# Window attention on TensorE row groups: row scores of all four head pairs in one piece, V first in a step, and finer waits for the next image

## The chip, the cores and the metric

The kernel runs on one core of a Trainium2 chip. The metric is device time in microseconds (us), the median of several runs. Names of engines: TensorE (PE in the profile; PEld is its weight load), VectorE (DVE), ScalarE (ACT), GpSimd (POOL), SyncE (SP, which here issues all DMAs).

## The reference

The input x is 4 images of 128 channels, 112 x 112 pixels, in float32. It is normalised in 32 groups of 4 channels, rolled by (-3, -3), projected to q, k and v (one 128 x 128 matrix each, with bias), cut into windows of 7 x 7 = 49 tokens, and each window attends within itself with 8 heads of 16 channels. The result is rolled back and added to x.

```python
qkv = jnp.einsum('bchw,oc->bohw', xs, w_qkv) + b_qkv[None, :, None, None]   # xs: normalised, rolled
...
scores = jnp.einsum('bxyhqd,bxyhkd->bxyhqk', q, k) * scale
attn = jax.nn.softmax(scores, axis=-1)
out = jnp.einsum('bxyhqk,bxyhkd->bxyhqd', attn, v)
...
x = x + _L0_conv_ref(_gn(x), L0_conv_w_qkv, L0_conv_b_qkv)
```

## The kernel before

An image is 16 bands of 7 rows; a band is 16 windows, handled as two groups of 8. That makes 128 groups, g = 0 to 127, and every engine runs one step for each g. The work of a group is spread over steps: its projection and its maxima stand in step g, its softmax in step g+1, its weighting and output in steps g+2 and g+3. Five programs are written out by hand, one for each engine; each runs its own list in order, and semaphores, which count groups, join them. Nothing is scheduled by a planner, so what an engine waits for is always its next instruction in the list.

In step g, before the change:

- TensorE: `sum_keys(g-2)` (L773, the denominators), `weigh(g-2)` (L785, probabilities times V), `project_v(g)` (L705), `turn_max(g-1)` (L734, transposes the negated row maxima), `column_scores(g-1, u=0)` (L760: `scores_of_keys` L746 and then `less_maximum` L755, which subtracts the maxima), `row_scores(g, 0)` (L719), `spread_inverse(g-2)` (L798), `project_k(g+1)` (L692), `column_scores(g-1, u=1)` (first L755, then L746), `row_scores(g, 1)`, `project_q(g+1)` (L699).
- ACT: `evac_q(g)` (L364), `normalise(g+2)` (L352), `evac_even(g-2)` (L392), `high_inverse(g-2)` (L386), `evac_neg(g-1)` (L370), `evac_v(g)` (L381), `exp(g-1, 0)` (L375), `evac_k(g+1)` (L359), `exp(g-1, 1)`.
- DVE: `low_q(g)`, `invert(g-2)`, `mask_q(g)`, `low_inverse(g-2)` (L581), `join(g-2)` (L590), `maximum(g, 0)` (L571), a chunk of the next image's statistics (`take_stats`, L491), `scale_rows(g-2)` (L597), `maximum(g, 1)`.
- POOL: `split_max(g-1)`, `add_image(g-3)`, `split_x(g+2)`, `split_k(g+1)`.

The scores are made twice: once with queries on the partitions (`row_scores`, 100 rows by 49 keys), only to find each row's maximum, and once with keys on the partitions (`column_scores`), which the exponential reads. A row score is one matmul that uses 32 rows of the array (the 32 channels of a pair of heads) and all 128 columns, with 49 moving columns. There are 8 windows, 3 products of high and low halves, and 4 head pairs h: 96 matmuls in a step. Head pair h lies on array rows 32h to 32h+31. Before the change each call handles two head pairs, which write two PSUM banks (0 and 1), and the second call waits until DVE has read the maxima of the first:

```python
wait(pe, max_done[1 - j], g + j)
for w in range(GW):
    for n, (low, k) in enumerate(((0, k_hi), (0, k_lo), (Q_LEN, k_hi))):
        for h in (2 * j, 2 * j + 1):
```

PSUM has 8 banks: 0 and 1 row scores (bank 0 also the turned maxima), 2 and 3 column scores (3 also the denominators), 4 Q and K, 5 V and the spread inverse, 6 and 7 the weighted result (`OUT_BANKS`), which `evac_even` and `join` read.

SP stores a finished band and then loads the band of the image after next into the freed slot. DVE takes the statistics of image b+1 while image b is worked on, 28 chunks of 448 pixels. After a change of image, in step 32b+2, DVE waits for all 16 bands of image b+1 (`dve.wait_ge(loaded[b + 1], 32 * BANDS)`), the last of which is loaded only when the last band of image b-1 has been stored.

## Time and profile before

| | |
|---|---|
| median of 3 runs | 1049.76 us (1048.53 to 1051.95) |
| profiled execution, its own time | 1047.67 us |
| its span, first to last instruction | 1045.9 us |
| mean granted TensorE clock | 0.970 |
| PE busy | 976.6 us (93%), 46595 matmuls |
| DVE busy | 785.8 us (75%) |
| ACT busy | 697.1 us (67%) |
| POOL busy | 595.6 us (57%) |
| HBM read and written | 25.89 MB and 25.69 MB |

The busy times are unions of the records of an engine over the whole span. The matmuls' records overlap, since a record holds the pipeline's latency as well as the stream of columns; the distance between starts tells what a matmul costs TensorE. The three runs lie 3.4 us apart (0.3%).

### The profile page before, as it was taken

The page shows a single profiled execution, that of the slowest core. Times are in us where ns is not written, and L with a number is a line of the kernel's source. Part 1 is how long each engine was busy: PE and PEld are TensorE (multiplying, and loading weights), DVE is VectorE, ACT ScalarE, POOL GpSimd, SP SyncE. Part 2 cuts the span into 40 slices and gives each one's busy share as a digit, 9 for nine tenths or more (in the row PEclk, how much of TensorE's full clock was granted, in tenths as well). Part 3 has the DMA queues.
Part 4 walks back from the last instruction along what each step waited for, and adds up shares of the span by engine and source line. Part 5 has one row for each costly group of instructions (what it writes and reads, how often), then busy time and mean ns, then how long its engine had stood idle before and what let it go on. Part 6 is the DMA issues. An engine that isn't in the chain of part 4 may idle for free. (4 is left out here: it accounts for less than half of the span.)

```text
span 1045.9 us, 104658 instructions
## 1 busy us (share of the span) xinstructions
PE 976.6 (93%) x46595; PEld 770.2 (74%) x46595; DVE 785.8 (75%) x1532; ACT 697.1 (67%) x1297; POOL 595.6 (57%) x1067
## 2 busy tenths in 40 slices
PE   0589999999979999999997999999999999999995
PEld 0367777777767777777775777787878787777774
DVE  7656888889856888888984888788877777777762
ACT  2455777777756777777774777777777777777752
POOL 1444666666555665666663666566656665666651
PEclk9988999999998999999997999999999999999995
DMA  9201111111110111111110000000000000000000
GB/s 382 119 18 52 47 45 61 61 54 39 61 62 31 61 40 53 61 61 46 46 62 31 31 31 15 31 31 31 15 31 31 31 19 27 31 31 24 22 33 34
DMA packets 29925, 52.05 MB, mean 50 GB/s; under 512 B 3650, under 2 KB 28868, under 8 KB 29764
## 3 DMA queue, kind: packets, MB, share of 16 engines
q1 hardware_dynamic: 29892, 51.59, 14.0%
q8 instruction: 23, 0.38, 0.2%
q14 instruction: 10, 0.08, 0.0%
HBM read 25.89 MB, written 25.69 MB: 49 GB/s over the span
## 5 line engine op out<-in xcount | busy, mean ns | idle before, releaser
L571 DVE TENSOR_REDUCE neg_max<-psum 100x16 f32<-100x784 f32 x256 | 249.5, 975 | 172.3 <-PE psum L729 172.3
L375 ACT ACTIVATE probs_t<-psum,exp_scale 128x800 f32<-128x800 f32 x256 | 237.5, 928 | 85.6 <-PE psum L746 55.4
L283 POOL TENSOR_SCALAR k_hi<-k 128x392 f16<-128x392 f32 x128 | 67.5, 527 | 243.3 <-PE psum L746 242.0
L746 PE MATMUL psum<-q_masks,k_hi 32*64 32x100 f16 x8192 | 190.3, 208 | 15.8 <-DVE inv L576 12.4
L729 PE MATMUL psum<-k_hi,q_masks 32*128 32x49 f16 x8192 | 199.2, 180 | 2.3 <-issue 1.2
L305 POOL TENSOR_TENSOR stage<-mixed,image 128x343 f32 (+7 forms) x256 | 162.4, 653 | 48.4 <-issue 37.4
L729 PEld LDWEIGHTS psum<-k_hi,q_masks 32*128 32x128 f16 x8192 | 176.4, 91 | 12.0 <-issue 1.6
L729 PE MATMUL psum<-k_lo,q_masks 32*128 32x49 f16 x4096 | 183.6, 179 | 0.6 <-issue 0.6
L746 PEld LDWEIGHTS psum<-q_masks,k_hi 32*64 32x64 f16 x8192 | 153.7, 106 | 39.1 <-issue 16.9
L564 DVE TENSOR_SCALAR q_masks<-q_halves,even_odd 128x800 f16<-128x800 f16 x256 | 162.8, 678 | 0.1
L729 PEld LDWEIGHTS psum<-k_lo,q_masks 32*128 32x128 f16 x4096 | 161.8, 92 | 0.8 <-issue 0.8
L746 PE MATMUL psum<-q_masks,k_lo 32*64 32x100 f16 x4096 | 160.7, 205 | 0.7 <-issue 0.7
L352 ACT ACTIVATE xn<-image,shift_c,rstd_c 128x21 f32 (+6 forms) x256 | 131.4, 564 | 8.8 <-DVE exp_scale L479 7.0
L793 PE MATMUL psum<-probs_t,v_rows 64*32 64x100 f32 x8192 | 133.3, 255 | 2.8 <-issue 2.8
L779 PEld LDWEIGHTS psum<-probs_t,sum_rows 128*32 128x32 f32 x8192 | 102.3, 112 | 45.0 <-issue 44.9
L285 POOL TENSOR_TENSOR k_lo<-k,k_hi 128x392 f16<-128x392 f32 x128 | 116.3, 909 | 10.7
L275 POOL TENSOR_TENSOR xn_lo<-xn,xn_hi 128x392 f16<-128x392 f32 x128 | 116.3, 908 | 10.7
L779 PE MATMUL psum<-probs_t,sum_rows 128*32 128x49 f32 x8192 | 120.1, 211 | 1.6 <-ACT probs_t L375 1.1
L746 PEld LDWEIGHTS psum<-q_masks,k_lo 32*64 32x64 f16 x4096 | 120.1, 107 | 1.0 <-issue 1.0
L556 DVE SCALAR_TENSOR_TENSOR q_halves<-psum,q_bias,q_halves 128x392 f16<-128x392 f32 x128 | 80.4, 628 | 51.7 <-ACT q_halves L364 36.6
L359 ACT ACTIVATE k<-psum,k_bias 128x392 f32<-128x392 f32 x128 | 75.2, 588 | 65.1 <-PE psum L696 65.1
L392 ACT ACTIVATE even_out<-psum,v_scale 128x392 f32<-128x392 f32 x128 | 75.2, 587 | 57.1 <-PE psum L793 57.1
(120 smaller groups left out, 1909.9 us busy)
## 6 DMA issues: line engine op xcount, KB each, us to landing
out_dram<-stage SPq DMA_DIRECT2D x64, 224.0 KB, 2.0
out_dram<-stage SPq DMA_DIRECT2D x64, 168.0 KB, 1.9
image<-in_x_dram SPq DMA_DIRECT2D x32, 224.0 KB, 2.6
image<-in_x_dram SPq DMA_DIRECT2D x1, 6104.0 KB, 27.2
image<-in_x_dram SPq DMA_DIRECT2D x34, 168.0 KB, 2.5
image<-in_x_dram SPq DMA_DIRECT2D x6, 896.0 KB, 9.4
image<-in_x_dram SPq DMA_DIRECT2D x1, 728.0 KB, 14.0
w_nat<-in_L_conv_w_qkv_dram SPq DMA_DIRECT2D x1, 192.0 KB, 2.5
```

The costliest lines, as they stand in the source:

```text
L275: nc.gpsimd.tensor_tensor(xn_lo[:, par, :, 0:TOK], xn[:, :, :], xn_hi[:, par, :, 0:TOK], ALU.subtract).then_inc(x_split, 1)
L285: nc.gpsimd.tensor_tensor(k_lo[:, par, :, 0:TOK], k, k_hi[:, par, :, 0:TOK], ALU.subtract).then_inc(k_split, 1)
L305: last = nc.gpsimd.tensor_tensor(pixel_view(stage[:, bass.ds(st, BAND)], piece), token_view(mixed[:, half, :, :], piece), pixel_view(image ...
L352: last = nc.scalar.activation(token_view(xn, piece), pixel_view(image[:, bass.ds(at, BAND)], piece), ACT.Identity, bias=shift_c[:, 0:1], s ...
L375: nc.scalar.activation(probs_t[:, 2 * u:2 * u + 2, :, :].rearrange("p h a q -> p h (a q)"), psum[:, COL_BANKS, 0:PAIRS * ROWS2], ACT.Exp, ...
L556: nc.vector.scalar_tensor_tensor(q_halves[:, 1, :, 0:TOK], psum[:, QK_BANK, 0:GT].rearrange("p (w q) -> p w q", q=TOK), q_bias[:, 0:1], q_ ...
L564: last = nc.vector.tensor_scalar(both[:, :, e, :], q_halves[:, :, :, :].rearrange("p l w q -> p (l w) q"), even_odd[:, e:e + 1], None, ALU ...
L571: nc.vector.tensor_reduce(neg_max[:, par, 2 * j:2 * j + 2, :], psum[0:ROWS2, ROW_BANKS, 0:GT] .rearrange("p h (w k) -> p h w k", k=TOK), A ...
L729: last = nc.tensor.matmul(psum[:, ROW_BANKS.start + h - 2 * j, w * TOK:(w + 1) * TOK], q_masks[rows, par, low + w * ROWS2:low + w * ROWS2 ...
L746: last = nc.tensor.matmul(psum[side, COL_BANKS.start + h % 2, a * ROWS2:(a + 1) * ROWS2], k[rows, par, w, :], q_masks[rows, par, low + w * ...
L779: last = nc.tensor.matmul(psum[c * PC:(c + 1) * PC, SUM_BANK, SPARE_SUM], sum_rows[:, a, e, :, :, :].rearrange("p t w s -> p (t w s)"), pr ...
L793: last = nc.tensor.matmul(psum[c * PC:(c + 1) * PC, OUT_BANKS.start + s, a * ROWS2:(a + 1) * ROWS2], v_rows[side, par, a, c * PC:(c + 1) * ...
```

## The change

- `row_scores(g)` is one call over all four head pairs. Pairs 0 and 1 write banks 6 and 7, pairs 2 and 3 banks 0 and 1. Since banks 6 and 7 also hold the weighted result, `row_scores(g)` waits for `join(g-2)`, and `weigh(g-2)` waits for `maximum(g-1, 0)`. (DVE raises `join_done` and `mixed_done` once at the start, so that their counts are one higher everywhere.)
- TensorE's list: `project_v(g)` comes first in a step, then `sum_keys` and `weigh`; `row_scores(g)` stands behind `project_k(g+1)`.
- ACT's list: `evac_v(g)` comes second. DVE's list: statistics and `scale_rows` stand ahead of both maxima.
- At an image change DVE's waits for loaded bands are cut in four, each for the bands that the next two chunks need; the wait for all 16 comes in step 32b+6 in place of 32b+2.
- At the start ACT waits for `scales_ready` only after its first step, statistics begin in step 2 rather than 1, and TensorE's loop begins at step 2, not 4, so that two steps less are written out.

```diff
@@ window_attention
-        ROW_BANKS, COL_BANKS, OUT_BANKS = slice(0, 2), slice(2, 4), slice(6, 8)
+        ROW_BANKS, COL_BANKS, OUT_BANKS = (slice(6, 8), slice(0, 2)), slice(2, 4), slice(6, 8)
...
-        row_mm = [sem("row_mm_0"), sem("row_mm_1")]
+        row_mm = sem("row_mm")
@@ scalar (ACT)
-            act.wait_ge(scales_ready, 1)
-
...
             def step(g, n, par):
                 if live(g):
                     evac_q(g)
+                    evac_v(g, par)
                 if live(g + 2):
                     normalise(g + 2, n + 1, par)
                 if live(g - 2):
...
                     high_inverse(g - 2)
                 if live(g - 1):
                     evac_neg(g - 1)
-                if live(g):
-                    evac_v(g, par)
-                if live(g - 1):
                     exp(g - 1, 0)
...
             act.wait_ge(norm_ready, 1)
-            for g in range(-2, 4):
+            step(-2, -1, 0)
+            act.wait_ge(scales_ready, 1)
+            for g in range(-1, 4):
                 step(g, g // 2, g & 1)
@@ vector (DVE)
+            dve.sem_inc(join_done, 1)
+            dve.sem_inc(mixed_done, 1)
...
             def maximum(g, par, j):
-                dve.wait_ge(row_mm[j], g + 1)
+                dve.wait_ge(row_mm, g + 1)
                 wait(dve, neg_split, g - 1)
-                nc.vector.tensor_reduce(neg_max[:, par, 2 * j:2 * j + 2, :], psum[0:ROWS2, ROW_BANKS, 0:GT]
+                nc.vector.tensor_reduce(neg_max[:, par, 2 * j:2 * j + 2, :], psum[0:ROWS2, ROW_BANKS[j], 0:GT]
...
                     join(g - 2)
                 if before:
                     before()
+                for chunk in chunks:
+                    take_stats(image_at + chunk * STAT, chunk)
+                if live(g - 2):
+                    scale_rows(g - 2, par)
+                if after:
+                    after()
                 if live(g):
                     maximum(g, par, 0)
-                for chunk in chunks:
-                    take_stats(image_at + chunk * STAT, chunk)
-                if after:
-                    after()
-                if live(g - 2):
-                    scale_rows(g - 2, par)
-                if live(g):
                     maximum(g, par, 1)
...
             step(0, 0, 0)
+            step(1, 0, 1)
             dve.wait_ge(loaded[1], 32)
-            step(1, 0, 1, (0, 1), BANDS * BAND)
-            step(2, 1, 0, (2, 3), BANDS * BAND)
-            step(3, 1, 1, (4, 5), BANDS * BAND)
+            step(2, 1, 0, (0, 1, 2), BANDS * BAND)
+            step(3, 1, 1, (3, 4, 5), BANDS * BAND)
...
-                dve.wait_ge(loaded[b + 1], 32 * -(-2 * STAT // BAND))
-                two_steps(first, 0, at)
-                dve.wait_ge(loaded[b + 1], 32 * -(-4 * STAT // BAND))
-                two_steps(first + 1, 2, at)
+                for n in range(4):
+                    dve.wait_ge(loaded[b + 1], 32 * -(-(2 * n + 2) * STAT // BAND))
+                    two_steps(first + n, 2 * n, at)
                 dve.wait_ge(loaded[b + 1], 32 * BANDS)
-                with dve.Fori(2, CHUNKS // 2) as n:
+                with dve.Fori(4, CHUNKS // 2) as n:
                     two_steps(n + first, 2 * n, at)
@@ tensor (PE)
-            def row_scores(g, par, j):
-
-                if j == 0:
-                    pe.wait_ge(q_masked, g + 1)
-                    pe.wait_ge(k_split, g + 1)
-                wait(pe, max_done[1 - j], g + j)
+            def row_scores(g, par):
+                pe.wait_ge(q_masked, g + 1)
+                pe.wait_ge(k_split, g + 1)
+                wait(pe, max_done[1], g)
+                wait(pe, join_done, g)
                 for w in range(GW):
                     for n, (low, k) in enumerate(((0, k_hi), (0, k_lo), (Q_LEN, k_hi))):
-                        for h in (2 * j, 2 * j + 1):
+                        for h in range(HP):
                             rows = slice(h * PC, (h + 1) * PC)
-                            last = nc.tensor.matmul(psum[:, ROW_BANKS.start + h - 2 * j, w * TOK:(w + 1) * TOK],
+                            last = nc.tensor.matmul(psum[:, ROW_BANKS[h // 2].start + h % 2, w * TOK:(w + 1) * TOK],
...
             def weigh(g, par):
                 pe.wait_ge(v_evac, g + 1)
-                wait(pe, join_done, g)
+                pe.wait_ge(max_done[0], min(g + 2, GROUPS) if isinstance(g, int) else g + 2)
+                wait(pe, join_done, g + 1)
...
+                if live(g):
+                    project_v(g, par)
                 if live(g - 2):
                     sum_keys(g - 2)
                     weigh(g - 2, par)
-                if live(g):
-                    project_v(g, par)
                 if live(g - 1):
                     turn_max(g - 1)
                     column_scores(g - 1, 1 - par, 0)
-                if live(g):
-                    row_scores(g, par, 0)
                 if live(g - 2):
                     spread_inverse(g - 2, live(g))
                 if live(g + 1):
                     project_k(g + 1, 1 - par)
+                if live(g):
+                    row_scores(g, par)
                 if live(g - 1):
                     column_scores(g - 1, 1 - par, 1)
-                if live(g):
-                    row_scores(g, par, 1)
                 if live(g + 1):
                     project_q(g + 1, 1 - par)
 
-            for g in range(-1, 4):
+            for g in range(-1, 2):
                 step(g, g & 1)
-            with pe.Fori(2, GROUPS // 2 - 1) as n:
+            with pe.Fori(1, GROUPS // 2 - 1) as n:
```

TensorE, loop body, before: from the end of `column_scores(g-1, 0)` to `column_scores(g-1, 1)`. L755 is `less_maximum`, L729 `row_scores`, L805 `spread_inverse`, L696 `project_k`. The brackets name the semaphores waited for.

```order
L755 MATMUL psum<-neg_rows,pick_window 128x100 [waits neg_ready]
L755 MATMUL psum<-neg_rows,pick_window 128x100 x7
L729 MATMUL psum<-k_hi,q_masks 128x49 [waits max_done_1,k_split,q_masked]
L729 MATMUL psum<-k_hi,q_masks 128x49
L729 MATMUL psum<-k_lo,q_masks 128x49 x2
L729 MATMUL psum<-k_hi,q_masks 128x49 x4
...
L805 MATMUL psum<-inv_rows,pick_head 128x49 [waits v_evac,inv_split]
L805 MATMUL psum<-inv_rows,pick_head 128x49 x7
```

The same place after the change (L752, L803, L694 and L726 are the same four functions):

```order
L752 MATMUL psum<-neg_rows,pick_window 128x100 [waits neg_ready]
L752 MATMUL psum<-neg_rows,pick_window 128x100 x7
L799 REGISTER_ALU [waits inv_split]
L803 MATMUL psum<-inv_rows,pick_head 128x49 [waits v_evac]
L803 MATMUL psum<-inv_rows,pick_head 128x49 x7
...
L726 MATMUL psum<-k_hi,q_masks 128x49 [waits max_done_1,join_done,k_split,q_masked]
L726 MATMUL psum<-k_hi,q_masks 128x49 x3
L726 MATMUL psum<-k_lo,q_masks 128x49 x4
L726 MATMUL psum<-k_hi,q_masks 128x49 x8
...
L752 MATMUL psum<-neg_rows,pick_window 128x100 [waits exp_done_0]
```

The row scores moved behind `project_k`, are issued in fours in place of twos, and gained the wait for `join_done`.

TensorE at the start of a step, before: `sum_keys` L779, `weigh` L793, `project_v` L710 and L714, `turn_max` L736.

```order
L779 MATMUL psum<-probs_t,sum_rows 32x49 [waits exp_done_1,exp_done_0]
L779 MATMUL psum<-probs_t,sum_rows 32x49 x31
L793 MATMUL psum<-probs_t,v_rows 32x100 [waits v_evac,join_done]
L793 MATMUL psum<-probs_t,v_rows 32x100 x31
L710 MATMUL psum<-bias_rows,ones_rows 128x512 [waits mixed_done,v_evac]
...
L736 MATMUL psum<-ident,neg_halves 128x100 [waits neg_split]
```

And after (`project_v` L708, `sum_keys` L776, `weigh` L791, `turn_max` L733, first row of `scores_of_keys` L743):

```order
L708 MATMUL psum<-bias_rows,ones_rows 128x512 [waits mixed_done,v_evac]
...
L776 MATMUL psum<-probs_t,sum_rows 32x49 [waits exp_done_1,exp_done_0]
L776 MATMUL psum<-probs_t,sum_rows 32x49 x31
L791 MATMUL psum<-probs_t,v_rows 32x100 [waits join_done,v_evac,max_done_0]
L791 MATMUL psum<-probs_t,v_rows 32x100 x31
L733 MATMUL psum<-ident16,neg_halves 128x100 [waits neg_split]
L743 MATMUL psum<-q_masks,k_hi 64x100 [waits inv_done,exp_done_1]
```

`project_v` no longer lies between `weigh` and `turn_max`; `weigh` now also waits for the first maxima of the group before.

ACT, one step of its loop, before and then after (L392/L390 `evac_even`, L386/L384 `high_inverse`, L370/L368 `evac_neg`, L381/L379 `evac_v`):

```order
L392 ACTIVATE even_out<-psum,v_scale 128x392 [waits join_done,out_mm]
L386 CAST inv_hi<-inv 128x49 [waits inv_split,inv_done]
L370 CAST neg_rows<-psum 128x100 [waits col_mm_1,neg_mm]
L381 COPY v_rows<-psum 128x512 [waits out_mm,v_mm]
L375 ACTIVATE probs_t<-psum,exp_scale 128x800 [waits out_mm,col_mm_0]
```

```order
L379 COPY v_rows<-psum 128x512 [waits out_mm,v_mm]
...
L390 ACTIVATE even_out<-psum,v_scale 128x392 [waits join_done,out_mm]
L384 CAST inv_hi<-inv 128x49 [waits inv_split,inv_done]
L368 CAST neg_rows<-psum 128x100 [waits col_mm_1,neg_mm]
L373 ACTIVATE probs_t<-psum,exp_scale 128x800 [waits out_mm,col_mm_0]
```

`evac_v` left its place between `evac_neg` and the exponential; `evac_even` and `high_inverse` still stand ahead of `evac_neg`.

## Rows read from the trace of the kernel before

**Rows 1.** Busy time in a stretch: us, then PE, PEld, DVE, ACT, POOL, clock, DMA
```profile
600.00:1000.00 400.00, 400.00 (x19600) 317.02 (x19606) 311.49 (x585) 290.46 (x538) 248.85 (x431) 1.00 0.07 27
```

**Rows 2.** Source line L710 (once a step), 600 to 1000 us: first and last start
```profile
L710 PE MATMUL psum<-bias_rows,ones_rows x54: 390/390/390, 599.8 to 993.4; 128*128 128x512 f16 x54
```

**Rows 3.** Timeline of TensorE, one step: start, us, engine, line, operation
```profile
857.97 0.91 PE L779 MATMUL psum<-probs_t,sum_rows 128*32 128x49 f32 x64
858.81 1.02 PE L793 MATMUL psum<-probs_t,v_rows 64*32 64x100 f32 x64
859.76 0.39 PE L710 MATMUL psum<-bias_rows,ones_rows 128*128 128x512 f16 x1
...
860.65 0.21 PE L736 MATMUL psum<-ident,neg_halves 100*128 100x100 bf16 x1
860.79 0.24 PE L746 MATMUL psum<-q_masks,k_hi 32*64 32x100 f16 x4
...
861.45 0.35 PE L755 MATMUL psum<-neg_rows,pick_window 32*128 32x100 bf16 x8
861.63 0.19 PE L729 MATMUL psum<-k_hi,q_masks 32*128 32x49 f16 x2
...
862.21 0.18 PE L729 MATMUL psum<-k_hi,q_masks 32*128 32x49 f16 x2
862.33 0.37 PE L805 MATMUL psum<-inv_rows,pick_head 128*128 128x49 f16 x8
862.54 0.33 PE L696 MATMUL psum<-xn_hi,w_hi 128*128 128x392 f16 x1
...
863.14 0.35 PE L755 MATMUL psum<-neg_rows,pick_window 32*128 32x100 bf16 x8
863.42 0.24 PE L746 MATMUL psum<-q_masks,k_hi 32*64 32x100 f16 x4
...
864.08 0.20 PE L729 MATMUL psum<-k_hi,q_masks 32*128 32x49 f16 x2
...
864.78 0.34 PE L702 MATMUL psum<-xn_hi,w_hi 128*128 128x392 f16 x1
...
865.40 0.29 PE L779 MATMUL psum<-probs_t,sum_rows 128*32 128x49 f32 x8
```

**Rows 4.** Timeline of ACT in the same step
```profile
859.94 0.59 ACT L392 ACTIVATE even_out<-psum,v_scale 128x392 f32<-128x392 f32 x1 [0.64 <-PE psum L793]
860.43 0.23 ACT L386 CAST inv_hi<-inv 128x49 f16<-128x49 f32 x1
860.90 0.24 ACT L370 CAST neg_rows<-psum 128x100 bf16<-128x100 f32 x1 [0.25 <-PE psum L736]
861.04 0.59 ACT L381 COPY v_rows<-psum 128x512 f32<-128x512 f32 x1
861.84 0.93 ACT L375 ACTIVATE probs_t<-psum,exp_scale 128x800 f32<-128x800 f32 x1 [0.21 <-PE psum L755]
```

**Rows 5.** Timeline of DVE in the same step
```profile
860.84 0.26 DVE L581 SCALAR_TENSOR_TENSOR inv_rows<-inv_hi,low_rows,inv 128x49 f16<-128x49 f16 x1
861.02 0.74 DVE L590 SCALAR_TENSOR_TENSOR summed<-psum,v_scale,even_out 128x196 f32<-128x196 f32 x2
```

**Rows 6.** Image changes: DVE's timeline at the first; L710 at first and second
```profile
310.64 0.63 DVE L556 SCALAR_TENSOR_TENSOR q_halves<-psum,q_bias,q_halves 128x392 f16<-128x392 f32 x1 [7.45 <-DMA image<-in_x_dram]
...
L710 PE MATMUL psum<-bias_rows,ones_rows x2: 389/389/389, 304.5 to 321.9; 128*128 128x512 f16 x2
...
L710 PE MATMUL psum<-bias_rows,ones_rows x3: 390/390/390, 544.7 to 570.1; 128*128 128x512 f16 x3
```

**Rows 7.** Start of the kernel: source line L710, first seven steps
```profile
L710 PE MATMUL psum<-bias_rows,ones_rows x7: 389/390/627, 39.1 to 96.6; 128*128 128x512 f16 x7
```

**Rows 8.** Busy time in stretches, columns as in the first group
```profile
75.00:81.00 6.00, 5.05 (x215) 3.81 (x203) 3.61 (x9) 2.96 (x6) 2.51 (x5) 1.00 0.44 136
...
82.00:88.00 6.00, 5.96 (x213) 4.65 (x213) 2.65 (x5) 2.71 (x5) 2.88 (x5) 0.50 0.02 6
```

More of the change, by code:

```diff
@@ L389, in evac_even @@
                 act.wait_ge(out_mm, g + 1)
-                wait(act, join_done, g)
+                wait(act, join_done, g + 1)
                 even = psum[:, OUT_BANKS, 0:PAIRS * ROWS2].rearrange("p s (a e q) -> p s a e q", e=2, q=QP)[:, :, :, 0, 0:TOK]
@@ L585, in join @@
                 dve.wait_ge(even_done, g + 1)
-                wait(dve, mixed_done, g)
+                wait(dve, mixed_done, g + 1)
                 by_side = summed[:, :, :].rearrange("p (a s) q -> p s a q", s=2)
@@ L802, in spread_inverse @@
                 else:
[L803 removed]
+                    pe.wait_ge(mixed_done, g + 1)
                 for w in range(GW):
```

9 lines of the change are left out of this document (4 added, 5 removed).

## The prediction

> **What bounds the kernel now.** I read the busy times of a quiet stretch first. Between 600 and 1000 us TensorE is busy for 400.00 of 400 us at granted clock 1.00, DVE for 311.49, ACT for 290.46 [rows 1]. So TensorE sets the pace there, and DVE, which needs 78% of a step, could follow a step of 5.8 us. The length of a step comes from a line that is issued once in each: L710 starts 54 times from 599.8 to 993.4, 53 steps of 7.43 us [rows 2]. Then I read TensorE's timeline for one step, by distances between starts, since these and not the records' lengths are what it pays [rows 3]. Block by block: sum_keys 0.84, weigh 0.95, project_v 0.89, turn_max 0.14, keys of column score 0 0.66, its less_maximum 0.18, row score 0 0.70, spread_inverse and project_k together 0.81, less_maximum 0.28, keys of column score 1 0.66, row score 1 0.70, project_q 0.62. The sum is 7.43, with no wait in it.
>
> The span of 1045.9 us is then: 118 steps of 7.43, two long ones at image changes, a slow start and a tail. The profiled execution took 1047.7 us; the median of the runs is 2.1 us above it, which I add at the end.
>
> **Row scores in fours.** One piece has 48 matmuls, in pairs on two groups of 32 array rows. The first pair starts at 861.63 and the 24th at 862.21, so 23 pairs take 0.58 us: 25 ns a pair [rows 3]. The next block, which uses the array in another shape, starts 0.12 after the last pair, 0.10 more than a pair needs. I count 0.10 for such a change of shape, included in the blocks above.
>
> After the change the 96 matmuls are 24 fours. What a four costs no row shows. Below: 25 ns, if four row groups run beside each other as two do now. Above: 50 ns, if nothing is won over two pairs, and more if four outputs at once get in each other's way. Three neighbours speak for the low end. spread_inverse issues 8 matmuls of the same 49 columns with full 128 x 128 weights in 0.21 us, 26 ns each [rows 3], so the weights of all four row groups go in within 26 ns. The keys of a column score are 48 matmuls in 0.66 less 0.10, that is 11.7 ns each, with 100 columns and four tiles beside each other [rows 3]; so issuing costs at most 11.7 ns and four would be at most 47. And the columns alone, 49 at 2.4 GHz, need 20.4 ns, the same for two or four groups. I take 25 ns: row scores cost 24 x 0.025 = 0.60 in place of 1.20.
>
> A rule speaks against this. The Trainium skill, TensorEngine Tiling, section Instruction Overhead, says that each matmul has an overhead of some 60 cycles and that a tiling factor should not be taken from a dimension that is already small. Our 49 columns are such a dimension, and 60 cycles are 25 ns. The trace agrees on the size, but shows it for a pair and not for one matmul [rows 3], so the floor is one of a row group. By the rule, paid matmul after matmul, the row scores would take 2.4 us and the sum would come to some 1200 us, which two groups already contradict.
>
> **Changes of shape.** Before there are ten in a step. After, row score and less_maximum (both 32 x 128) and project_q and project_v (both full) are neighbours, and project_v parts from turn_max by sum_keys and weigh: nine. That saves 0.10. TensorE's own work falls to 7.43 - 0.60 - 0.10 = 6.73 us.
>
> **The wait that takes its place.** project_v used to stand between weigh and turn_max and gave ACT 0.89 us in which to get through. Count from the start of the new step, at project_v. It takes 0.89 + 0.10 (shape), sum_keys until 1.83, weigh until 2.78, turn_max until 2.92, keys of column score 0 until 3.58. There less_maximum needs neg_rows from ACT. evac_even starts 1.13 us after weigh starts (859.94 less 858.81), so at 2.96; high_inverse follows 0.49 later at 3.45; evac_neg can follow 0.14 after that (the distance of two such short instructions is that of 860.90 and 861.04) and lasts 0.24: 3.83 [rows 3, 4]. A semaphore's reach from TensorE to ACT is 0.04 (turn_max ends at 860.86, evac_neg starts at 860.90) and I take 0.05 for the way back: 3.88. TensorE waits 0.30 us, in every step. Moving evac_v ahead does not help here, since evac_even waits for weigh and not for ACT.
>
> What follows is not late. less_maximum lasts 0.18 + 0.10, until 4.16. spread_inverse needs DVE's low_inverse: inv_hi is done at 3.68, low_inverse starts at 3.72 and ends at 3.98 [rows 4, 5]. Then 0.81 until 4.97. There the new wait for join: join starts 0.18 after low_inverse, 3.90, and ends at 4.64 [rows 5], 0.33 early. Behind the row scores (5.57) column score 1 needs the first exponential: it starts 0.39 after less_maximum starts (861.84 less 861.45) and lasts 0.93, so it ends at 5.20 [rows 3, 4], 0.37 early. Then 0.28, 0.66 and project_q with 0.62 less 0.10: the step ends at **7.03 us**, 0.40 less than now. DVE's 5.8 us with the statistics ahead of the maxima fit: all of its list but the maxima lies beside TensorE's first 5.6 us, and the maxima beside column score 1, project_q and the next project_v. weigh's new wait, for a maximum that is read some 2 us after the row scores, ends before the 1.83 + 7.03 - 5.57 = 3.3 us that TensorE takes to get there.
>
> **Image changes.** DVE waits 7.45 us for the DMA at the first, and L710, normally 7.43 apart, is 17.4 apart there; at the second, two periods take 25.4 [rows 6]. Beyond a normal step that is 10.0 and 10.5, wait and slow restart together. In the new code the wait for all bands stands four steps (28 us) later, and the bands of the first four waits were loaded long before. The third change has no such wait. I take all 20.5 us as gained. The instructions that merge statistics stand ahead of the maxima now; they have the slack of DVE, some 1.2 us a step, and I count them at nothing (at most 1 us for each of three changes).
>
> **Start.** The first six periods of L710 take 57.5 us against 44.6 for six normal ones: 12.9 too many [rows 7]. Part of it is code that is met for the first time, which before are steps 0 to 3 written out and then two of the loop, and after 0 and 1 and two of the loop. I take a third of 12.9 as gained, 4.3 (estimate; 0 to 10). ACT's later wait and the rest of the DVE prologue: not counted, under 1 us.
>
> **Sum.** Steps: 118 normal ones and the six first, 124 x 0.40 = 49.6. Image changes 20.5. Start 4.3. In all 74.4: 1047.7 - 74.4 = 973.3, and with the 2.1 of the median **975 us**.
>
> **Rivals.** The fixed part, 24.8 us, holds in all of them; what differs is the step, P, and the time is 1049.8 - 24.8 - 124 x (7.43 - P).
>
> - The main case: P from 6.93 to 7.15, 963 to 990 us with the steps alone, 956 with a start at its better end. Chance 0.72.
> - Fours at 25 ns, but another wait of 0.1 to 0.4 us in each step. The list of candidates is above: join has 0.33 of slack, the exponential 0.37, low_inverse 0.18, and ACT's three-piece normalise of every other group lies just ahead of evac_even. P 7.15 to 7.45: 990 to 1027 us. 0.14.
> - Four row groups win little: a four at 47 to 50 ns. P is 7.03 + 24 x 0.025 = 7.63 at 50, and the 0.20 that each step loses eats exactly the fixed part: 1050 us. At 47 it is 1041. For it speaks that no row has more than two groups of rows writing all 128 columns at once. 0.07.
> - The other side: the two further groups are served in turn, one after the other, behind the first pair, since each of the four writes every partition of PSUM. A four then costs 25 + 25 + 25 = 75 ns, row scores 1.80, P = 8.23: 1124 us. It decides from 50 ns a four on. Against it: two groups that write all partitions show no such price. 0.04.
> - The clock. Now 84% busy at 75 to 81 us is followed by 0.50 of the clock at 82 to 88, where 6 us hold 213 matmuls against 49 a microsecond in the quiet stretch [rows 1, 8]. The new step leaves TensorE idle for 0.30 of 7.03 us, 96% busy. Should 0.50 be granted in the middle of the run, a step takes about 1.4 times as long by these counts (35 a microsecond), 3 us more; from 25 such steps on the gain is gone. The Trainium skill, TensorE: Matmul & The Clock Gate, Part 1, tells of a kernel whose frequent short idle times between groups of matmuls made the clock swing. 0.03.
>
> **How the numbers follow.** Faster by over 0.3% (about what a measurement of this kernel can tell from no change): the first two and most of the third, 0.91. Within 0.3%: the top of the third, 0.02. Slower: the last two, 0.07. The range takes in the main case and the nearer half of the second: 956 to 1006 us, 0.80.
>
> **What the new profile would show.** Right: 96 row-score matmuls within 0.60 us, starts of fours 25 ns apart; L708 starting every 7.03 us; before L752, the first less_maximum of a step, an idle time of TensorE's weight load of 0.3 us ended by ACT's neg_rows; no DVE wait for a DMA at the image changes and steps there as long as others; granted clock 1.00 from the fourth step on. The prediction is wrong if fours are 40 ns or more apart, if the wait stands before L726 with DVE's summed as its releaser, or if the clock row of the quiet stretch is below 1.00.

## The result, and the profile after

The changed kernel takes 1367.03 us (median of 4 runs, 1366.01 to 1369.11), the kernel before 1050.12 beside it. The ratio is 1.302, between 1.299 and 1.305: 317 us slower, where 75 us faster was forecast. The forecast missed by 392 us. One of the four runs of e6 below took 1532.40 us, for a reason that nothing here shows; it is part of e6's median of 1011.41 us, which would be 1010.94 without it, and its ratio leaves it out.

The page of the kernel after, its span, busy times and clock row:

```profile
span 1363.9 us, 104634 instructions
PE 1115.8 (82%) x46595; PEld 847.6 (62%) x46595; DVE 751.7 (55%) x1532; ACT 668.7 (49%) x1297; POOL 588.0 (43%) x1067
PEclk9887787787787787787787787787787787787786
```

The same work stands there, 46595 matmuls, but no engine is full. The clock row is the surprise: 7 and 8 through the whole run. Busy time in the stretch that [rows 1] showed full (us; then PE, PEld, DVE, ACT, POOL, clock, DMA):

```profile
600.00:1000.00 400.00, 338.02 (x14213) 257.35 (x14214) 230.13 (x478) 203.00 (x396) 179.23 (x315) 0.80 0.07 26
```

TensorE is idle for 62 of 400 us, and the clock granted to it averages 0.80. `project_v`'s first matmul, once a step, from 600 to 900 us:

```profile
L708 PE MATMUL psum<-bias_rows,ones_rows x29: 377/378/628, 604.8 to 891.6; 128*128 128x512 f16 x29
```

29 starts from 604.8 to 891.6 are 28 steps of 10.24 us, against 7.43 [rows 2] and 7.03 forecast. The waits of the whole run: engine, line and what it waited for, then us in total, times, longest us (three rows of the list):

```profile
ACT v_rows L379 <- PE psum L791: 336.0, 126, 3.8
DVE inv_rows L581 <- ACT inv_hi L384: 237.4, 128, 2.9
PE psum L752 <- ACT neg_rows L368: 193.5, 125, 1.9
```

The three rows belong together. ACT stands for 336 us, 2.7 us in each step, before `evac_v`, until TensorE's `weigh` (L791) is done. So what ACT does behind it, `inv_hi` and `neg_rows` among it, comes late. DVE waits for `inv_hi`, and TensorE stands before `less_maximum` (L752) for `neg_rows`, 1.55 us a step. It is the only wait that TensorE has in every step. Here is ACT's timeline: start, us, engine, line, operation, and in brackets the idle time ahead and what ended it:

```profile
607.71 0.58 ACT L379 COPY v_rows<-psum 128x512 f32<-128x512 f32 x1 [1.86 <-PE psum L791]
608.19 0.75 ACT L350 ACTIVATE xn<-image,shift_c,rstd_c 128x392 f32 x1
608.84 0.58 ACT L390 ACTIVATE even_out<-psum,v_scale 128x392 f32<-128x392 f32 x1
609.31 0.23 ACT L384 CAST inv_hi<-inv 128x49 f16<-128x49 f32 x1
609.43 0.25 ACT L368 CAST neg_rows<-psum 128x100 bf16<-128x100 f32 x1
...
618.86 0.58 ACT L379 COPY v_rows<-psum 128x512 f32<-128x512 f32 x1 [3.61 <-PE psum L791]
619.34 1.30 ACT L350 ACTIVATE xn<-image,shift_c,rstd_c 128x343 f32 x3
...
621.13 0.24 ACT L368 CAST neg_rows<-psum 128x100 bf16<-128x100 f32 x1
```

And TensorE's, from the row scores ahead of the first of these steps on, with the wait of the second step as its last row:

```profile
602.62 0.20 PE L726 MATMUL psum<-k_hi,q_masks 32*128 32x49 f16 x4
602.68 0.21 PE L726 MATMUL psum<-k_hi,q_masks 32*128 32x49 f16 x8
...
603.39 0.34 PE L752 MATMUL psum<-neg_rows,pick_window 32*128 32x100 bf16 x8
...
606.66 1.02 PE L791 MATMUL psum<-probs_t,v_rows 64*32 64x100 f32 x64
607.61 0.22 PE L733 MATMUL psum<-ident,neg_halves 100*128 100x100 bf16 x1
...
609.74 0.35 PE L752 MATMUL psum<-neg_rows,pick_window 32*128 32x100 bf16 x8 [1.26 <-ACT neg_rows L368]
...
621.43 0.52 PE L752 MATMUL psum<-neg_rows,pick_window 32*128 32x100 bf16 x8 [1.86 <-ACT neg_rows L368]
```

Read the two together. `weigh` has issued its last matmul when `turn_max` starts at 607.61, and `evac_v` starts 0.10 later, 607.71. In [rows 4] it was `evac_even` that started at `weigh`'s end. Now `evac_v` (0.48 until the next start), `normalise` (0.65) and `evac_even` (0.47) stand in a row between `weigh` and `neg_rows`, and in every other group `normalise` has three pieces and takes 1.30, so that the wait is 1.86 and not 1.26. `evac_v(g)` waits for `weigh(g-2)` since `v_rows` has two buffers and `weigh` reads the one that is overwritten: `wait(act, out_mm, g - 1)`. That wait was there before too, but there it stood behind `evac_even`, which waits for the same event, and cost nothing.

Also seen here: 96 row-score matmuls take 0.77 us (602.62 to 603.39), not 0.60. Stretches of 3 us show how the clock goes in the middle of the run, columns as above:

```profile
612.00:615.00 3.00, 3.00 (x69) 1.90 (x60) 1.85 (x2) 1.26 (x2) 1.18 (x2) 0.50 0.19 69
...
618.00:621.00 3.00, 1.57 (x113) 1.23 (x89) 0.91 (x3) 2.14 (x5) 0.13 (x1) 1.00 0.00 0
```

0.50, the lower of the two levels (1.2 GHz), is granted from 612 to 615 us, behind the wait that ends at 609.74, and 1.00 (2.4 GHz) is back at 618 to 621; the kernel before kept 1.00 in its quiet stretch [rows 1].

### The profile page after: what moved, and what is told of

The parts are those of the page before. It is cut to its first block and busy times, and to the rows that moved or that the text cites. A ratio compares the mean times of both kernels' runs of the same rounds, so it can differ in the third digit from the quotient of the medians.

```text
span 1363.9 us, 104634 instructions
## 1 busy us (share of the span) xinstructions
PE 1115.8 (82%) x46595; PEld 847.6 (62%) x46595; DVE 751.7 (55%) x1532; ACT 668.7 (49%) x1297; POOL 588.0 (43%) x1067
## 5 line engine op out<-in xcount | busy, mean ns | idle before, releaser
L752 PE MATMUL psum<-neg_rows,pick_window 32*128 32x100 bf16 x2048 | 108.9, 238 | 194.1 <-ACT neg_rows L368 193.5
L379 ACT COPY v_rows<-psum 128x512 f32<-128x512 f32 x128 | 74.9, 585 | 337.4 <-PE psum L791 336.0
L743 PE MATMUL psum<-q_masks,k_hi 32*64 32x100 f16 x8192 | 217.1, 225 | 3.3 <-issue 3.3
L752 PEld LDWEIGHTS psum<-neg_rows,pick_window 32*128 32x128 bf16 x2048 | 66.7, 109 | 211.4 <-ACT neg_rows L368 210.5
L743 PEld LDWEIGHTS psum<-q_masks,k_hi 32*64 32x64 f16 x8192 | 177.7, 119 | 27.0 <-issue 7.4
L273 POOL TENSOR_SCALAR xn_hi<-xn 128x392 f16<-128x392 f32 x128 | 67.4, 527 | 292.0 <-ACT xn L350 292.0
L743 PE MATMUL psum<-q_masks,k_lo 32*64 32x100 f16 x4096 | 184.1, 222 | 1.0 <-issue 1.0
L581 DVE SCALAR_TENSOR_TENSOR inv_rows<-inv_hi,low_rows,inv 128x49 f16<-128x49 f16 x128 | 35.1, 274 | 237.4 <-ACT inv_hi L384 237.4
L726 PEld LDWEIGHTS psum<-k_hi,q_masks 32*128 32x128 f16 x8192 | 125.4, 106 | 63.2 <-issue 62.6
L776 PE MATMUL psum<-probs_t,sum_rows 128*32 128x49 f32 x8192 | 146.4, 237 | 2.2 <-ACT probs_t L373 2.2
L726 PE MATMUL psum<-k_hi,q_masks 32*128 32x49 f16 x8192 | 141.7, 205 | 2.1 <-issue 2.1
L776 PEld LDWEIGHTS psum<-probs_t,sum_rows 128*32 128x32 f32 x8192 | 127.2, 132 | 21.5 <-issue 15.0
L791 PE MATMUL psum<-probs_t,v_rows 64*32 64x100 f32 x8192 | 134.3, 256 | 0.3 <-issue 0.3
L576 DVE RECIPROCAL inv<-psum 128x49 f32<-128x49 f32 x128 | 60.1, 470 | 134.6 <-PE psum L776 134.6
L743 PEld LDWEIGHTS psum<-q_masks,k_lo 32*64 32x64 f16 x4096 | 132.3, 119 | 1.1 <-issue 1.1
L726 PE MATMUL psum<-k_lo,q_masks 32*128 32x49 f16 x4096 | 131.1, 204 | 2.0 <-issue 2.0
```

Of the source, the lines that this page charges most:

```text
L273: nc.gpsimd.tensor_scalar(xn_hi[:, par, :, 0:TOK], xn[:, :, :], 1.0, 0.0, ALU.mult, ALU.add).then_inc(x_high, 1)
L379: nc.scalar.copy(v_rows[:, par, :, :].rearrange("p a d -> p (a d)"), psum[:, V_BANK, :]).then_inc(v_evac, 1)
L726: last = nc.tensor.matmul(psum[:, ROW_BANKS[h // 2].start + h % 2, w * TOK:(w + 1) * TOK], q_masks[rows, par, low + w * ROWS2:low + w * RO ...
L743: last = nc.tensor.matmul(psum[side, COL_BANKS.start + h % 2, a * ROWS2:(a + 1) * ROWS2], k[rows, par, w, :], q_masks[rows, par, low + w * ...
L752: last = nc.tensor.matmul(psum[:, COL_BANKS.start + h % 2, a * ROWS2:(a + 1) * ROWS2], pick_window[rows, 2 * a:2 * a + 2, :].rearrange("p ...
L776: last = nc.tensor.matmul(psum[c * PC:(c + 1) * PC, SUM_BANK, SPARE_SUM], sum_rows[:, a, e, :, :, :].rearrange("p t w s -> p (t w s)"), pr ...
```

## Experiments

The theory after the result (A): the wait for `out_mm`, moved ahead of `normalise`, `evac_even` and `evac_neg` with `evac_v`, makes TensorE idle, and the idle time costs the clock. Rivals: (B) ACT merely has more work ahead of `neg_rows`, the wait is nothing; (C) four row groups at once are slow; (D) the new waits that tie `weigh` and `row_scores` to DVE's maxima and `join`. In each diff "-" is the kernel that it starts from. Ratios are to the kernel before, run beside it, with their 95% interval.

**e1, the copy back.** The changed kernel, with ACT's `evac_v` where it stood before.

```diff
                     evac_q(g)
-                    evac_v(g, par)
...
                     evac_neg(g - 1)
+                if live(g):
+                    evac_v(g, par)
```

> The changed kernel with one thing undone: ACT's evac_v stands behind evac_neg again, as before the change. Theory (ACT): in the changed order evac_v is ACT's second instruction and waits not only for project_v but, by its wait for out_mm, for weigh of the group two back, whose buffer it overwrites; normalise, evac_even, high_inverse and evac_neg queue behind it, so that TensorE waits 1.3 us (even groups) or 1.9 us (odd groups) in front of less_maximum, and these idle times make the granted clock fall. With evac_v back, the wait before less_maximum should be 0.3 us, one of 0.2 us should appear before spread_inverse (it needs evac_v), the step should be 7.4 us and the clock 1.00 in the middle of the run: 1022 us, 1010 to 1040. Rival (row groups): the clock falls because four row groups run at once, whatever ACT does: clock stays near 0.80, the step above 8.5 us, time above 1180.

Measured: 1038.28 us, 0.9884 (0.9866 to 0.9903). One line moved takes off 329 us, so (C) and (D) are out as causes of the loss. The stretch of 600 to 900 us, then who waited before `less_maximum`, then the first matmul of `project_v`:

```profile
600.00:900.00 300.00, 279.12 (x14444) 217.38 (x14437) 251.25 (x439) 203.56 (x398) 183.20 (x319) 1.00 0.07 27
...
PEld psum L754 <- ACT neg_rows L368: 10.8, 39, 0.3
...
L710 PE MATMUL psum<-bias_rows,ones_rows x40: 377/377/378, 601.2 to 896.3; 128*128 128x512 f16 x40
```

The wait of 0.30 that the prediction worked out is there: 10.8 us in 39 steps. But the step is 7.57, not 7.03, and my 1022 was missed. Single steps alternate between 7.31 and 7.84. The cause of the long ones shows below (e8).

**e11, the wait alone.** e1, and at the place where the changed kernel has `evac_v`, ACT waits for the same semaphore and copies nothing.

```diff
                     evac_q(g)
+                    wait(act, out_mm, g - 1)
+                    act.sem_inc(waited_act, 1)
```

> The copy-back kernel (evac_v behind evac_neg, 1038 us) with the wait alone put where the change puts it: ACT waits for weigh of the group two back behind evac_q, without copying anything there. Theory (the wait and what queues behind it): normalise, evac_even, high_inverse and evac_neg start only after weigh, the wait before less_maximum is 0.9 us (even groups) and 1.5 (odd), the clock falls below 0.95 and the time is above 1150 us. Rival (the half microsecond of the copy and its place): no change, 1030 to 1050 us.

Measured: 1367.11 us, 1.3025 (1.300 to 1.305), the changed kernel's time. The busy row, then `turn_max` and `normalise` in one step, then the waits of the next:

```profile
600.00:900.00 300.00, 254.97 (x10695) 192.79 (x10699) 174.47 (x348) 151.76 (x292) 132.58 (x234) 0.79 0.08 28
...
607.41 0.22 PE L737 MATMUL psum<-ident,neg_halves 100*128 100x100 bf16 x1
607.89 0.75 ACT L350 ACTIVATE xn<-image,shift_c,rstd_c 128x392 f32 x1 [2.23 <-PE psum L795]
...
620.97 0.35 PE L756 MATMUL psum<-neg_rows,pick_window 32*128 32x100 bf16 x8 [1.56 <-ACT neg_rows L368]
621.54 0.36 PE L807 MATMUL psum<-inv_rows,pick_head 128*128 128x49 f16 x8 [0.22 <-ACT v_rows L379]
```

So the wait gives the loss without the copy, and (B), by which the wait is nothing, is out. It doesn't follow that the copy's 0.48 us is worth nothing. Nothing is copied here ahead of `normalise`, and yet it starts 0.48 after `turn_max` (607.41 to 607.89), where the changed kernel has 0.58 (607.61 to 608.19): the bare wait takes most of the copy's time. And the copy, now behind `neg_rows`, makes `spread_inverse` wait for `v_rows`. That the two times agree so closely is in part luck. What the copy is worth shows in e3.

**e2, four buffers.** The wait goes away by rights when `v_rows` has four buffers, since then `weigh(g-4)` frees the one that is written.

```diff
-        v_rows = sb("v_rows", [C, 2, PAIRS, C])
+        v_rows = sb("v_rows", [C, 4, PAIRS, C])
...
-                wait(act, out_mm, g - 1)
+                wait(act, out_mm, g - 3)
...
-            with pe.Fori(1, GROUPS // 2 - 1) as n:
-                step(2 * n, 0)
-                step(2 * n + 1, 1)
+            with pe.Fori(0, (GROUPS // 2 - 2) // 2) as m:
+                for i in range(4):
+                    step(4 * m + 2 + i, i & 1, i)
```

> The changed kernel in its own order, but v_rows has four buffers in place of two, so that evac_v of a group waits for weigh of four groups back and not of two (loops of ACT and TensorE hold four steps instead of two). Theory (ACT's wait): evac_v no longer waits for TensorE's weigh of this step; wait before less_maximum 0.3 us for even and odd groups alike, step 7.2 us, clock 1.00: 997 us, 985 to 1015. Rival (position): the copy's place and its 0.5 us on ACT make less_maximum late even without the wait: a wait above 0.7 us, step above 7.6, time above 1046. Rival (row groups): clock near 0.80 and above 1180 us.

Measured: 1571.86 us, 1.494 (1.490 to 1.498). This run doesn't decide what it was made for, since it changed something else. Its queue that loads instructions (packets, MB, share), and two of TensorE's waits over the whole run, at the row scores and before `less_maximum`:

```profile
q8 instruction: 413, 6.77, 1.9%
...
PE psum L730 <- issue: 108.9, 92, 2.5
...
PE psum L756 <- ACT neg_rows L368: 6.7, 39, 0.2
```

In the changed kernel that queue has 17 packets and 0.28 MB and the wait for "issue" at the row scores is 4.0 us in place of 108.9. The buffer's number is a constant in this kernel's code, so the loops hold four steps in place of two; that TensorE's longer body is loaded anew in each pass is my reading of the 6.77 MB. The wait for `neg_rows` does fall from 193.5 to 6.7 us, but TensorE is itself late here, which gives ACT time. How much of the run's time is the loading stays open.

**e3, normalise first.** The changed kernel with `evac_v` behind `normalise`, so that this is done by the time `weigh` ends.

```diff
                     evac_q(g)
-                    evac_v(g, par)
                 if live(g + 2):
                     normalise(g + 2, n + 1, par)
+                if live(g):
+                    evac_v(g, par)
```

> The changed kernel with normalise ahead of evac_v on ACT, a smaller dose: normalise runs while evac_v's wait for weigh lasts, but evac_v itself (0.49 us) still stands ahead of evac_even and evac_neg. Theory: wait before less_maximum 0.8 us for even and odd groups alike, a tenth of a step. If TensorE keeps its clock at 10% idle time, the step is 7.7 us and the time 1058 (1045 to 1075); if the clock falls at 10% too, it is above 1150. Rival (row groups): same clock, near 0.80, as the changed kernel.

Measured: 1147.9 us, 1.0932 (1.091 to 1.095).

```profile
600.00:900.00 300.00, 265.76 (x12932) 205.72 (x12920) 229.24 (x405) 183.44 (x354) 162.80 (x284) 0.93 0.06 23
...
PE psum L753 <- ACT neg_rows L368: 23.0, 35, 0.7
```

The wait before `less_maximum` falls to 0.66 us a step, and the clock comes back to 0.93, between my two cases (1058 with it, over 1150 without). Less than half of that wait is left, and 219 us of the time are gone. Beside e1 this is the price of the copy. Here `evac_v` waits for the same `weigh` as the `evac_even` behind it, so all that its place adds is 0.48 us ahead of `neg_rows`, and e3 takes 110 us more than e1. Taken in this order, and with what the clock makes of them, the 329 us have two parts: 110 for the copy in that place, and 219 for the wait that pushes `normalise` behind `weigh`.

**e5, filler.** What is the clock's share? The changed kernel, with 28 matmuls that write unused columns of a bank, placed ahead of the wait before `less_maximum`. They compute nothing, and hold TensorE busy while `neg_rows` is late (the wait for `q_low` is there so that nothing else uses the bank).

```diff
+                        pe.wait_ge(q_low, g + 2)
+                        for _ in range(FILL):
+                            nc.tensor.matmul(psum[:, QK_BANK, GT:GT + ROWS2], w_hi[:, 1, :], w_hi[:, 0, 0:ROWS2], ...)
```

> The changed kernel with 28 extra matmuls a step on TensorE (full array, 100 columns, into free columns of the Q/K bank, result unused), issued just ahead of less_maximum's wait for ACT, some 1.25 us of work that lies inside the time in which TensorE waits there anyway. It adds work and removes none. Theory (idle time sets the clock): the clock stays at 1.00, the wait left is 0 to 0.1 us (even groups) and 0.6 us (odd), the step is 8.5 us on average and the time 1160 us (1130 to 1190), some 200 faster than the changed kernel by doing more. Rival (row groups or load make the clock fall): clock 0.80 or lower and 1367 us or more.

Measured: 1161.26 us, 1.1057 (1.104 to 1.108).

```profile
600.00:900.00 300.00, 290.58 (x13792) 236.51 (x13775) 211.52 (x404) 178.29 (x353) 160.66 (x282) 1.00 0.07 24
...
608.98 0.22 PE L734 MATMUL psum<-ident,neg_halves 100*128 100x100 bf16 x1
...
609.78 1.41 PE L766 MATMUL psum<-w_hi 128*128 128x100 f16 x28
611.12 0.35 PE L753 MATMUL psum<-neg_rows,pick_window 32*128 32x100 bf16 x8
...
L709 PE MATMUL psum<-bias_rows,ones_rows x35: 377/377/377, 606.2 to 896.2; 128*128 128x512 f16 x35
```

More work takes 206 us off. The clock is 1.00, and the step, 34 in 290.0 us, is 8.53. The filler takes next to no time of its own: `less_maximum` starts 2.14 after `turn_max` (608.98 to 611.12), in the changed kernel 2.13 (607.61 to 609.74). So of the 392 us of the miss, 206 are the clock; a step of 8.53 in place of 7.03 is the rest, 124 x 1.50 = 186. Of the 1.50, the wait is 1.25 (1.55 less the 0.30 forecast) and the row scores 0.17; 0.08 I don't assign.

**e4, image changes alone.** The kernel before, with only DVE's finer waits for loaded bands.

```diff
-                dve.wait_ge(loaded[b + 1], 32 * -(-2 * STAT // BAND))
-                two_steps(first, 0, at)
-                dve.wait_ge(loaded[b + 1], 32 * -(-4 * STAT // BAND))
-                two_steps(first + 1, 2, at)
+                for n in range(4):
+                    dve.wait_ge(loaded[b + 1], 32 * -(-(2 * n + 2) * STAT // BAND))
+                    two_steps(first + n, 2 * n, at)
```

> The kernel before with the change's waits for loaded bands at an image change and nothing else of it. The prediction's term: the two long steps at image changes (10.0 and 10.5 us beyond a normal one) go entirely, 1050.5 - 20.5 = 1030 us (1027 to 1033). Rival: the wait is only put off, and DVE waits in step 32b+6 for the last band, or the merging of statistics becomes late: above 1040 us.

Measured: 1027.76 us, 0.9798 (0.976 to 0.983), 21.1 below the 1048.86 of the kernel before beside it. `project_v` at the first image change:

```profile
L709 PE MATMUL psum<-bias_rows,ones_rows x6: 389/389/389, 297.1 to 334.2; 128*128 128x512 f16 x6
```

Five steps of 7.42: the long one is gone. The term of 20.5 holds, and it is a gain by itself.

**e6, a new order.** Can the order of the whole be had without the wait? On ACT `evac_even` and `evac_v` go behind `evac_neg`, so nothing that waits for `weigh` stands ahead of it; on TensorE `project_k` goes ahead of `spread_inverse`, which then has 0.5 us more for `low_inverse`. From e1:

```diff
@@ scalar (ACT)
-                    evac_even(g - 2)
                     high_inverse(g - 2)
                 if live(g - 1):
                     evac_neg(g - 1)
+                if live(g - 2):
+                    evac_even(g - 2)
@@ tensor (PE)
-                if live(g - 2):
-                    spread_inverse(g - 2, live(g))
                 if live(g + 1):
                     project_k(g + 1, 1 - par)
+                if live(g - 2):
+                    spread_inverse(g - 2, live(g))
```

> The changed kernel with another order on ACT and one exchange on TensorE. ACT: evac_q, normalise, high_inverse, evac_neg, evac_even, evac_v, exp 0, evac_k, exp 1; TensorE: project_k ahead of spread_inverse. Neither evac_neg nor high_inverse stands behind an instruction that waits for weigh, and evac_v's half microsecond is over before spread_inverse, now later, needs it. Theory: no wait of TensorE above 0.1 us in a step, clock 1.00, a step of 6.9 us (6.73 and 0.17 for row scores that take 0.77 and not 0.60): 1050 - 25 - 124 x 0.5 = 963 us, 955 to 985. Rival (a chain that I don't see, or DVE held by GpSimd as in the copy-back run): a step above 7.2, above 996 us.

Measured: 1011.41 us, 0.9623 (0.958 to 0.967), against 963 expected. Steps alternate between 6.90 and 7.76: one in two is what was hoped for. In a long one TensorE waits twice for DVE, for `low_inverse` and then for `join`, which stands behind it in DVE's list:

```profile
611.69 0.37 PE L806 MATMUL psum<-inv_rows,pick_head 128*128 128x49 f16 x8 [0.26 <-DVE inv_rows L584]
612.44 0.20 PE L729 MATMUL psum<-k_hi,q_masks 32*128 32x49 f16 x4 [0.37 <-DVE summed L593]
```

**e8, GpSimd's reads.** The long steps of e1 and e6 have a long `low_inverse`. Here it is in a short and in a long step of e1, then what GpSimd does beside the long one, then TensorE behind it:

```profile
604.95 0.40 DVE L583 SCALAR_TENSOR_TENSOR inv_rows<-inv_hi,low_rows,inv 128x49 f16<-128x49 f16 x1 [0.24 <-ACT inv_hi L384]
...
612.38 0.92 DVE L583 SCALAR_TENSOR_TENSOR inv_rows<-inv_hi,low_rows,inv 128x49 f16<-128x49 f16 x1
...
612.32 0.91 POOL L275 TENSOR_TENSOR xn_lo<-xn,xn_hi 128x392 f16<-128x392 f32 x1
...
613.35 0.37 PE L805 MATMUL psum<-inv_rows,pick_head 128*128 128x49 f16 x8 [0.67 <-DVE inv_rows L583]
```

The same instruction took 0.26 in [rows 5]. The long one ends 0.07 after GpSimd's subtraction, and TensorE waits 0.67 for it. e8 is e1 with that subtraction done for one window of eight (the low half of the normalised input is zero in the others, so part of the products is left out).

```diff
-                nc.gpsimd.tensor_tensor(xn_lo[:, par, :, 0:TOK], xn[:, :, :], xn_hi[:, par, :, 0:TOK],
+                nc.gpsimd.tensor_tensor(xn_lo[:, par, 0:1, 0:TOK], xn[:, 0:1, :], xn_hi[:, par, 0:1, 0:TOK],
```

> The copy-back kernel with GpSimd's xn_lo subtraction done for one of the 8 windows only (the rest of the low half of x stays zero, which leaves a part of the products out). In the copy-back run every other step was 7.85 and not 7.31 us, and in it DVE's low_inverse took 0.92 us in place of 0.27 and ended 0.07 after GpSimd's xn_lo. Theory (a shared way to SBUF holds DVE while GpSimd reads): low_inverse takes 0.3 us in all steps, both kinds of step are 7.31, and the time is 124 x 0.27 less: 1005 us (998 to 1015). Rival (low_inverse is long for ACT's sake or for the odd groups' three-piece normalise): steps go on alternating and the time stays within 8 us of 1038.

Measured: 1013.95 us, 0.9674 (0.963 to 0.972), 24 below e1. The long steps go from 7.84 to 7.42. `low_inverse`, grouped by line (count, total us and mean ns of one; then idle ahead), in e1 and in e8:

```profile
L583 DVE SCALAR_TENSOR_TENSOR inv_rows<-inv_hi,low_rows,inv 128x49 f16<-128x49 f16 x128 | 81.6, 638 | 21.1 <-ACT inv_hi L384 20.6
```

```profile
L583 DVE SCALAR_TENSOR_TENSOR inv_rows<-inv_hi,low_rows,inv 128x49 f16<-128x49 f16 x128 | 45.9, 358 | 20.4 <-ACT inv_hi L384 19.9
```

The Trainium skill, SBUF — State Buffer, section Who interferes with whom, states that a DVE instruction with two SBUF inputs contends with a GpSimd instruction that reads SBUF, and that one with at most one such input doesn't, outside DVE's 2-port modes. The first half is what these rows show; the second half is a remedy, tried next.

**e10, the inverse in PSUM.** e6, with the reciprocals written to free columns of PSUM bank 1, so that `low_inverse` has one SBUF input.

```diff
-        inv32 = sb("inv32", [C, TOK])
+        inv32 = psum[:, 1, GT:GT + TOK]
```

> e6_new_order with the reciprocals of the denominators (inv32) in free columns of PSUM bank 1 in place of SBUF, so that DVE's low_inverse reads one input from SBUF and not two. In e6_new_order every other step was 7.76 and not 6.90 us, and in it low_inverse started 0.06 after GpSimd's xn_lo and ended 0.06 after it (0.92 us). Theory (DVE is held when it needs a second SBUF input while GpSimd reads): low_inverse takes 0.3 us throughout, all steps are 6.9 to 7.0 us, and the time is 124 x 0.43 = 53 us less than 1011: 960 (950 to 975). Rival: the odd step is long for another reason and the time stays above 1000.

Measured: 970.63 us, 0.9247 (0.923 to 0.926), the fastest of all and 79 us below the kernel before. `low_inverse` in e6 and then in e10:

```profile
L584 DVE SCALAR_TENSOR_TENSOR inv_rows<-inv_hi,low_rows,inv 128x49 f16<-128x49 f16 x128 | 72.2, 564 | 0.6 <-ACT inv_hi L384 0.6
```

```profile
L584 DVE SCALAR_TENSOR_TENSOR inv_rows<-inv_hi,low_rows,psum 128x49 f16<-128x49 f16 x128 | 32.6, 255 | 0.5 <-ACT inv_hi L384 0.5
```

From 564 to 255 ns, with GpSimd's work whole. Its stretch and steps:

```profile
600.00:900.00 300.00, 296.50 (x15628) 238.09 (x15616) 251.43 (x468) 215.73 (x430) 195.96 (x342) 1.00 0.08 28
...
L711 PE MATMUL psum<-bias_rows,ones_rows x42: 377/377/378, 605.8 to 893.1; 128*128 128x512 f16 x42
```

TensorE is busy for 296.50 of 300 us, and 41 steps take 287.3: 7.01 each. The expected 960 (950 to 975) was met.

**e7 and e9, pairs for fours.** What are the fours worth? e7 was to be e6 with the row scores in two runs of pairs, as the expectation says.

```diff
-                    for n, (low, k) in enumerate(((0, k_hi), (0, k_lo), (Q_LEN, k_hi))):
-                        for h in range(HP):
+                    for j, n, (low, k) in ((j, *t) for j in range(2) for t in enumerate(((0, k_hi), (0, k_lo), (Q_LEN, k_hi)))):
+                        for h in (2 * j, 2 * j + 1):
```

> The same kernel as e6_new_order, but the 96 row-score matmuls are issued in pairs (all of head pairs 0 and 1, then all of 2 and 3), in one piece. Theory: pairs cost 25 ns as before the change, 1.20 us in place of 0.77, TensorE is the bound, so the step is 0.43 longer than in e6_new_order and the time 50 us longer (40 to 60). Rival: the step is bound elsewhere, and fours gain less than 15 us over pairs.

Measured: 1013.83 us, 0.9657 (0.963 to 0.969), 2.4 above e6. That wasn't the experiment described: the pairs change inside each window, and one pair runs beside the other; the 96 matmuls took 0.80 us (601.39 to 602.19 in one step). e9 is the real one, on e10, with all of pairs 0 and 1 ahead of pairs 2 and 3:

```diff
-                for w in range(GW):
+                for j, w in ((j, w) for j in range(2) for w in range(GW)):
...
-                        for h in range(HP):
+                        for h in (2 * j, 2 * j + 1):
```

> e10_inverse_psum with the row scores as two runs of pairs, first all windows of head pairs 0 and 1, then all of 2 and 3, which is how the kernel before issues them; e7_pairs changed head pairs inside each window, so that pairs of different row groups still overlapped (its 96 matmuls took 0.79 us). Theory: 96 matmuls take 1.20 us at 25 ns a pair, TensorE is the bound and the step is 0.43 longer: 45 to 60 us more than e10_inverse_psum. Rival: less than 20 us more, fours do not pay.

Measured: 1015.32 us, 0.9668 (0.965 to 0.969), 44.7 above e10.

```profile
L711 PE MATMUL psum<-bias_rows,ones_rows x41: 377/377/378, 603.9 to 898.6; 128*128 128x512 f16 x41
```

Steps of 7.37 against 7.01. The fours are worth 0.36 a step, where 0.60 was forecast, and 44.7 us lies just under the 45 to 60 that I expected.

## Why the prediction was wrong

**The step that failed** is in the part on the wait: "Moving evac_v ahead does not help here, since evac_even waits for weigh and not for ACT." It looks at what `evac_v` leaves behind and not at what it takes along. The chain was started with `evac_even` 1.13 after `weigh` starts. In fact `evac_v` starts there, and `normalise` and `evac_even` follow: by [rows 4] and the rows above, 0.48 + 0.65 later in one group, more with three pieces. The 0.30 should have been about 1.4 and 2; measured are 1.26 and 1.86 in the two steps shown, and 1.55 over the run. The row that told it stood in the order shown ahead of the prediction, `L379 ... [waits out_mm,v_mm]`. The experiments bear it out: with `evac_v` back (e1) 329 us go, with only `normalise` taken out from behind the wait (e3) 219 of them, and the wait without the copy (e11) gives the changed kernel's time.

**The clock** was a rival at 0.03, and its condition was tied to my own 0.30. With a wait of that size the clock stays: e1 has it, and runs at 1.00. With the true wait the rival was the main case, and e5 gives it 206 us. It also came in another form than priced: not 0.50 throughout, but 0.50 and 1.00 in turn, 0.80 on average. The Trainium skill, TensorE: Matmul & The Clock Gate, Part 1, which the prediction cited on frequent short idle times, fits: no idle time before `less_maximum` is longer than 1.9 us here, or than 0.7 in e3, and the mean granted clock is 0.80 and 0.93.

**The fours** were sized too low: 0.77 us in place of 0.60, 24 x 0.007 a step. The row of 25 ns holds, but only for the first 8; then they come 33 ns apart (next section). That took 0.17 of the gain of 0.60 in each step, 21 us in all, and left 0.43; e9 found 0.36. The floor of 47 to 50 and the price of 75 ns were both far off, and so was a floor paid matmul after matmul, which would have made 2.4 us of the 0.77. I called 11.7 ns a matmul an upper bound on issuing, and took a value (6.3 ns) that no row had.

**What held.** The image changes: 21.1 measured in e4, 20.5 forecast. The wait before `less_maximum` once the copy is back: 0.28 in e1, 0.30 forecast. The new waits for `join` and the maxima, and the one for the exponential, did not bind in the changed kernel: over the whole run TensorE waited for the exponential 2.8 us and no row of its waits names `join` or the maxima. (In e6, behind the long `low_inverse`, `join` does bind, 0.37 in every other step.) The start: the seventh start of `project_v` came at 96.6 before [rows 7], and at 86.9 in e10; six steps that are 0.4 shorter give 2.4 of that 9.7, so 7 us against 4.3. That is e10 and not the changed kernel, and of the 7 us 1.3 lie ahead of the first start (39.1 and 37.8).

**What was missing** beside the fault: `low_inverse` at 0.26, read from one row, had 0.18 of slack. It became 0.92 in every other step of e1, since that order put it beside GpSimd's subtraction; in the changed kernel itself, where all of this comes later, it takes 0.27 on average. That is the rival of "another wait of 0.1 to 0.4 us", hidden under the greater loss. And by an accident of terms the version without both faults, e10, takes 970.63 us with steps of 7.01, near the 975 and 7.03 of the forecast: it has no wait of 0.30, but dearer row scores. The agreement is luck: e10 isn't the kernel that was forecast.

## What to carry to other kernels

When an instruction moves up its engine's list, read every semaphore in its brackets, those that free a buffer too, and let the chain of that engine start at the latest of them; whatever used to stand ahead of it now inherits that wait. When the sum then shows an idle time of TensorE of a microsecond in each step, price it twice, once for itself and once for the clock. And take an instruction's duration from all its instances and from who runs beside it in the new order, not from one row.

## What the runs showed of the hardware

- **Short idle time that comes back in every step lowers TensorE's mean clock**, by turns of 0.50 and 1.00. Busy share of 600 to 900 us and mean granted clock: 0.97 and 1.00 (e5), 0.93 and 1.00 (e1), 0.89 and 0.93 (e3), 0.85 and 0.79 (e11). The share alone doesn't give the clock: e2, whose idle time lies elsewhere in the step, has 0.74 and 0.80. Filler in the idle time gave 206 us back.
- **Row groups in fours start 25 ns apart at first, then 33.** In the row scores of the changed kernel:

```profile
602.76 0.21 PE L726 MATMUL psum<-k_hi,q_masks 32*128 32x49 f16 x8
...
603.05 0.25 PE L726 MATMUL psum<-k_hi,q_masks 32*128 32x49 f16 x8
603.15 0.25 PE L726 MATMUL psum<-k_hi,q_masks 32*128 32x49 f16 x8
```

  Rows of eight that follow each other start three fours apart. From 602.68 (in the result's rows) to 602.76 that is 0.08 us, 25 to 27 ns a four, and from 603.05 to 603.15 it is 0.10: 33 ns a four or 8.3 ns for a matmul with its weight load. That the issue of instructions is the limit there, with a stock of some 8 fours built up ahead, is my reading and was not tried by itself. The lengths of the records grow in the same rows.
- **GpSimd's reads stretch a DVE instruction with two SBUF inputs** from 0.26 to 0.92 us (e1), and an input in PSUM avoids it: 564 to 255 ns on average and 40.8 us of time between e6 and e10.
- **A longer loop body can cost instruction loading**: 6.77 MB of instructions with four steps in the bodies of TensorE and ACT (e2), 0.28 MB with two. Which engine's they are, the row of the queue doesn't say.
